# Two attentions of a four-layer kernel: products with the values in four blocks of one chunk of keys a group, in place of two blocks of two chunks

## What is computed

```python
# layer 2 (rope_ in the profile)
scores = einsum('bqhd,bkhd->bhqk', q, k) * scale
scores = where(causal, scores, -inf)
attn = softmax(scores, axis=-1)
ctx = einsum('bhqk,bkhd->bqhd', attn, v)
# layer 3 (ctx_ in the profile)
scores = einsum('bhqd,bhkd->bhqk', Q, K) * SCALE + 0.1 * influence[:, None]
attn = softmax(scores, axis=-1)
out = einsum('bhqk,bhkd->bhqd', attn, V)
```

## Time and profile before

| | |
|---|---|
| median of three runs | 1824.76 us (1817.14 to 1826.03) |
| the profiled execution | 1819.46 us, of which the span of instructions is 1817.7 |
| mean granted TensorE clock | 0.903 |
| TensorE matmuls busy | 1491.0 us (82%), 8757 records |
| TensorE weight loads busy | 881.8 us (49%) |
| VectorE busy | 1261.8 us (69%) |
| ScalarE busy | 1026.5 us (56%) |
| GpSimd busy | 825.7 us (45%) |
| products with the values, records | 1024 in rope, 1024 in ctx, all of L1717 |

### The profile page before, as it was taken

One profiled execution on the slowest core, in us unless ns is written; L12 is line 12 of the kernel. 1 busy time (PEld: TensorE's weight loads), 2 busy tenths in 40 slices (PEclk: granted clock), 3 DMA queues, 4 the chain that ended last, 5 costly groups with the idle time before them and its releaser, 6 DMA issues. The chain is left out here.

```text
span 1817.7 us, 26884 instructions
## 1 busy us (share of the span) xinstructions
PE 1491.0 (82%) x8757; PEld 881.8 (49%) x8757; DVE 1261.8 (69%) x3276; ACT 1026.5 (56%) x1749; POOL 825.7 (45%) x935
## 2 busy tenths in 40 slices
PE   3788888569998899587679999999995867999980
PEld 1444455334444444333245554555552745777770
DVE  1656667368888887368677777877872555888875
ACT  2444555326666666234546777767775634777762
POOL 1244534545666654425721121122002565688875
PEclk8889899769999999688869999999997878999995
DMA  7800000212222220000534444444420012344415
GB/s 210 269 14 1 1 1 1 61 56 76 72 76 70 71 75 25 17 1 1 114 86 128 124 106 108 120 120 122 98 50 24 21 60 84 116 125 138 128 54 139
DMA packets 104521, 143.77 MB, mean 79 GB/s; under 512 B 31906, under 2 KB 72867, under 8 KB 101808
## 3 DMA queue, kind: packets, MB, share of 16 engines
q1 hardware_dynamic: 99392, 133.59, 26.8%
q0 software_dynamic: 4992, 8.48, 1.4%
HBM read 103.93 MB, written 57.22 MB: 89 GB/s over the span
## 5 line engine op out<-in xcount | busy, mean ns | idle before, releaser
L1198 DVE TENSOR_REDUCE ctx_nm<-ctx_s 128x1 f32<-128x512 f32 x496 | 319.9, 680 | 87.1 <-PE ctx_s L1354 86.3
L1198 DVE TENSOR_REDUCE rope_nm<-rope_s 128x1 f32<-128x128 f32 x496 | 220.4, 479 | 63.1 <-PE rope_s L1357 61.4
L1598 ACT ACTIVATE rope_probs<-rope_st 128x1024 f32<-128x1024 f32 (+1 forms) x256 | 171.5, 702 | 122.8 <-PE rope_st L1701 121.4
L1598 ACT ACTIVATE ctx_probs<-ctx_st 128x1024 f32<-128x1024 f32 x192 | 190.3, 1023 | 87.1 <-PE ctx_st L1701 83.5
L1354 PE MATMUL ctx_s<-att_kst,att_qst 96*128 96x512 f32 x496 | 210.8, 458 | 19.3 <-DVE ctx_nm L1198 8.4
L1354 PE MATMUL rope_s<-att_kst,att_qst 96*128 96x128 bf16 x496 | 145.3, 312 | 25.9 <-DVE rope_nm L1198 12.7
L1701 PE MATMUL ctx_st<-att_qst,att_kst 98*128 98x512 f32 x512 | 164.4, 404 | 2.4 <-ACT ctx_probs L1598 1.5
L1354 PEld LDWEIGHTS ctx_s<-att_kst,att_qst 96*128 96x128 f32 x496 | 95.8, 193 | 126.9 <-DVE ctx_nm L1198 51.9
L1463 POOL TENSOR_SCALAR_AFFINE_SELECT rope_probs<-rope_probs 128x256 f32<-128x256 f32 x256 | 97.9, 410 | 114.9 <-ACT rope_probs L1598 113.8
L2970 DVE TENSOR_TENSOR sw_hf<-sw_silu,sw_u 128x512 f32<-128x512 f32 x124 | 84.6, 682 | 84.2 <-ACT sw_silu L2728 52.4
L2728 ACT ACTIVATE sw_silu<-sw_g 128x512 f32<-128x512 f32 x124 | 74.3, 599 | 117.7 <-PE sw_g L110 92.3
(11 more groups left out here) (435 smaller groups left out, 3507.0 us busy)
## 6 DMA issues: line engine op xcount, KB each, us to landing
sw_raw<-in_L_ffn_all SPq DMA_DIRECT2D x24, 768.0 KB
sw_xs<-in_pad SPq DMA_DIRECT2D x65, 260.0 KB, 10.6
ctx_halves<-att_qk SPq DMA_DIRECT2D x24, 512.0 KB, 5.7
att_qst<-ctx_contexts SPq DMA_DIRECT2D x32, 384.0 KB
att_kst<-ctx_contexts SPq DMA_DIRECT2D x32, 384.0 KB
rope_halves<-att_qk SPq DMA_DIRECT2D x32, 256.0 KB, 3.3
att_qst<-rope_halves SPq DMA_DIRECT2D x32, 192.0 KB, 3.0
att_kst<-rope_halves SPq DMA_DIRECT2D x32, 192.0 KB, 3.3
```

The lines of the kernel that those rows point to most:

```text
L1198: nc.vector.tensor_reduce(nm[:, g, j * T + t:j * T + t + 1], bank("s", b, n)[:, 0:keys], AXX, ALU.max, negate=True).then_inc(s_used, 1)
L1598: nc.scalar.activation(prob(n // GH % 2, n % GH)[:, u * units[0]:u * units[0] + units[u]], st_bank[u][:, 0:units[u]], ACT.Exp, scale=SCALE ...
```

## The change

`weigh_values` is called for chunk j after every odd step (h % 8 = 1, 3, 5, 7), one chunk each time, in place of chunks 0 and 1 after step 3 and chunks 2 and 3 after step 7. `weigh_values` itself, its waits, its increments and all other engines' programs stay as they are. The order among chunks is the same, so the sums are formed in the same order. The loop serves both attentions.

```diff
--- before.py
+++ after.py
@@ -1731,8 +1731,7 @@
                         scores_by_key(now[0], now[1] // 8, j, u)
                     if within(ahead[0]) and not lead(ahead):
                         score(*ahead, j, 2 * u + 1)
-                    if within(behind[0]) and u == 1 and j in (1, 3):
-                        weigh_values(*behind, j - 1)
+                    if within(behind[0]) and u == 1:
                         weigh_values(*behind, j)
                     if within(c) and c >= LEAD:
                         if h == AT["yT"]:
```

## The result

The changed kernel took 1811.88 us, the median of 13 runs (1802.87 to 1819.58), against 1819.7 (1814.51 to 1827.12, 13 runs) for the kernel before on the same chip: a ratio of 0.9949 (95% interval 0.9934 to 0.9964), 8 us less. The forecast was 20 us less. The sign was right, the size was not.

A forecast was written before the change was run, and what follows sets the result against it. TensorE and VectorE were taken to wait for each other in bursts. Borders of 4.7 us against 7.3 recovered (85% of 8.6) gave 2.6 a batch pair, times 7.75: -20 us, so 1800; forecast 1788 to 1814, range 1774 to 1830.

The forecast's parts named there:

- Ctx, borders: TensorE in ctx: each extra switch to 32-column matmuls and back costs 0.34 us, 2.7 us a batch for eight.
- Ctx, net -1.3 us a batch: Ctx attention: 2.7 us of added borders less 4.0 us of recovered TensorE stalls in each batch.
- the sum: Both stages over 7.75 batches: ctx -10, rope -20, -30 us in full; -20 us with 85% of recovery counted.
- Rope, borders: TensorE in rope: each extra switch of matmul mode and back costs 0.25 us, 2.0 us a batch.
- Rope, recovered 4.6 us a batch: TensorE in rope: the new blocks fill stalls for VectorE, the side bank and ScalarE, giving back 4.6 us a batch.
- The added wait, masks at step 1: Rope: the first chunk waits for GpSimd's last mask, 1.1 us once a batch, in place of a wait for VectorE.
- the rope term: Rope attention: net -2.6 us a batch, -20 us over 7.75 batches.
- 1 (borders tip the balance): Both attentions: waits move instead of shrinking, so extra borders become added time, 1834 to 1856 us; chance 0.14.
- 2: Rope: GpSimd's later masks hold two groups a batch about 1.2 us each, total 1811 to 1820 us; chance 0.17.
- 3: Both attentions: all waits between engines go, 12 us recovered a batch pair, about 1763 us; chance 0.06.
- 4: Whole kernel: nothing moves, time within 9 us of no change only by sums cancelling; chance 0.06.
- The signs: If right: VectorE's idle before scores down a third or more, batches about 43.5 (rope), 56.5 us (ctx); mask waits under 10.

The follow-up runs named there:

- borders_only: Kernel before, with one score tile placed between the two chunks of each value block in both attentions: +31.1 us, ratio 1.0183.
- ctx_only: Kernel before with one-chunk blocks in ctx alone, rope left as before: -11.4 us, ratio 0.9947.
- both_kfirst_masks: Changed kernel with the key stack loaded ahead of the guard and rope's last masks ahead of GpSimd's finish: -25.6 us against the kernel before, ratio 0.9850.
- before_kfirst: Kernel before with the key stack's load issued ahead of the guard's: -1.5 us, ratio 0.9992.
- ctx_kfirst: Kernel before with one-chunk blocks in ctx alone and key stacks loaded ahead of the guard: -15.4 us, ratio 0.9916.
- before_kfirst_2: Kernel before with the key stack's load ahead of the guard's, run again in a later group: -3.4 us, ratio 0.9977.
- rope_kfirst: Kernel before with one-chunk blocks in rope alone and key stacks loaded ahead of the guard: -7.3 us, ratio 0.9960.
- rope_only: Kernel before with one-chunk blocks in rope alone, ctx left as before: +3.2 us, ratio 1.0016.
- both_kfirst_masks_2: Changed kernel with early key stack load and rope's masks ahead of finish, run again: -28.4 us against the kernel before, ratio 0.9845.
- both_again: The changed kernel run once more for a second profile: -6.0 us against the kernel before, ratio 0.9968.
- both_kfirst: Changed kernel with the key stack's load issued ahead of the guard's: -20.7 us against the kernel before, ratio 0.9879.

## Why the prediction was right or wrong

1. *Ctx, borders* (0.34 us a pair): right, 0.337 after, 0.33 in borders_only.
2. *Ctx, net -1.3 us a batch*: right, though part of it needed the early load (loop -6 to -8 us without, -10 with). Typical periods of 56.1 to 56.5 against 57.57 are -1.1 to -1.5. The median of ctx_only, -11.4, lies beside the -10 in full of the sum. The half group of the earlier trace rows, 1165.35 to the block at 1169.14 and the score behind it at 1171.00, has its answer in the rows from 1163.35 to 1168.40: TensorE now has a block at 1163.35 where it stood still for VectorE.
3. *Rope, borders* (0.25): right in kind; borders_only's rope loop rose by 10 us for some 56 pairs, 0.18 each, and its typical period by 0.12 a pair, so part was covered.
4. *Rope, recovered 4.6 us a batch*: wrong, and this is the step that failed. It is so even with load and masks out of the way, where the typical period fell by 0.3 us (44.30 to 43.96 or 44.00) and not by 2.6. With eight pairs of borders at 0.12 (borders_only) to 0.25 us (the prediction's price) what came back is 1.3 to 2.3 us. Three things were wrong in the count. First, the items named in it sum to 3.9 at most (1.1 at 581.90, 1.0 at 595.34, three of 0.3, 0.9 before 607.25) and not to 4.6. Second, most of them did not go: TensorE's gaps in a quiet batch sum to 3.3 us before (491.71 to 536.01) and to 2.3 in both_kfirst_masks (487.33 to 531.33). The one of 0.95 for the side bank fell to 0.17, as foreseen, but the one of 0.67 for VectorE only to 0.59, and new ones of 0.24 and 0.26 for VectorE stand elsewhere. Third, the batch that I read was not typical. Distances between starts of L1253 in rope before are 43.2, 45.8, 44.3, 44.3 and 46.5 us; the quiet ones are 44.3 (all after the first in before_kfirst), and the one read was 45.78. The stall of 0.83 at 581.90, which I counted for every batch, occurs in two of them (the other at 447.53): VectorE's L1213 took 0.16 us in the batch before and 1.33 us in this one, while GpSimd ran a long operation (the order of time of VectorE twice, then of GpSimd, kernel before):

```profile
535.74 0.16 DVE L1213 TENSOR_TENSOR rope_cut<-rope_nm,rope_rounded 128x16 f32<-128x16 f32 x1
```

```profile
580.05 1.33 DVE L1213 TENSOR_TENSOR rope_cut<-rope_nm,rope_rounded 128x16 f32<-128x16 f32 x1
```

```profile
580.06 1.29 POOL L1107 TENSOR_TENSOR att_wide<-Y,att_twin 128x512 f32<-128x512 f32 x1
```

   Over rope's whole loop it is about 4 us less (303.3 and 305.5 against 308.2 to 308.9), where 2.6 x 7.75 = 20 was forecast. What sets 44.0 is open: VectorE was busy 152.1 of the 176.1 us of four batches (443.33 to 619.45 in both_kfirst_masks) and the weight loads of scores still waited 31.5 us for it.
5. *The added wait, masks at step 1 (1.1 us once a batch, hidden)*: place, size and cover right for a quiet batch. TensorE waits 0.73, 1.03, 0.73, 0.83 and 0.76 us at 480.71, 524.66, 568.21, 613.28 and 658.67 after, once a batch, where 1.1 was foreseen. The wait comes in place of one for VectorE (0.59 in both_kfirst_masks), and the typical period is the same with it and without. What wasn't foreseen is its cost outside of quiet batches: the slow clock behind some of these gaps, and 3 us or so at the end of the loop.
6. *What the sum didn't have*: the key stack's load. I followed what each engine waits for, and not what each would reach sooner. The step said of the moved products which waits come nearer (masks, bank, exponentials) and left out that shortening the block of chunks 2 and 3 at the group's end brings TensorE sooner to an operand whose load was 0.3 us from the edge before. It made 12 to 15 us of weight-load waits in rope and 5 to 9 us in ctx. It adds to the miss but isn't the step that failed: early loads take it away, and item 4 stays as it is. And not all of these waits cost time (see the periods after). The trace of before held the warning twice more, in waits of 5.29 us at 400.25 and of 1.11 at 625.06 for this very load:

```profile
400.25 0.29 PE L1354 MATMUL rope_s<-att_kst,att_qst 96*128 96x128 bf16 x1 [5.29 <-DMA att_kst<-rope_halves]
...
625.06 0.23 PE L1354 MATMUL rope_s<-att_kst,att_qst 96*128 96x128 bf16 x1 [1.11 <-DMA att_kst<-rope_halves]
```

7. *The total*: ctx -11, rope +3: -8. With the load early the kernel is 20.7 us under the one before, by chance the number forecast, with another split: ctx -12.0 (ctx_kfirst less before_kfirst_2), rope -3.9 (rope_kfirst less before_kfirst_2), the early load itself -1.5 to -3.4. It doesn't confirm the rope term.
8. *Rivals*: 1 (borders tip the balance) is false for ctx; rope alone is slower by a hair (+3.2, interval touching 1), but its typical period in rope_only is 43.96, so that comes with the waits for the load and the slow clock, not with the borders. 2 was the nearest to the result in time, 1811 to 1820, by luck: its wait is there, 0.7 to 1.1 us once a batch and not 2.4, and it was covered in quiet batches. 3 and 4 fell.
9. *The signs*: ctx's batch of 56.46, the pair of borders at 0.34 and 4.1 us of mask waits came as said. VectorE's idle time did not: it fell by 5% in rope (44.5 to 42.2) and 17% in ctx (73.9 to 61.2), where a third or more was named.

One difference is left open. By medians rope's change, with early load and masks, is worth 12.9 us (both_kfirst_masks_2 less ctx_kfirst), while its loop shows 4 to 5 us. About 4 of the missing 8 us are no time of the kernel: ctx_kfirst's profile is of its fastest execution (1782.56 us, 4.2 under its median). Of the 8.3 us between the two profiled executions 5.0 lie in rope's loop, 3.1 between rope's last score and ctx's first batch (228.6 and 225.5 us; 232.7 in before_kfirst_2) and 1.2 ahead of rope's loop, and ctx's loop and the rest give 1.0 back. These are differences of single profiles, and no run took the stretch between the loops apart. What the masks' move would give the kernel before was not tried either.

## What to carry to other kernels

When an edit makes an engine reach a point sooner, look at each operand of what stands next in its order and read how long before its use it landed: a load 0.3 us ahead of its user can be a wait after the edit. Read a gain from several periods of a stage, and take the most frequent, before you multiply one batch's stalls by the number of batches. And expect a gap that you fill to come back in part elsewhere: of 3.3 us of gaps in a quiet rope batch 1.0 went. And when two waits stand near each other, take both away before you judge either: early masks alone only lengthened the wait for the keys here, and with the early load they brought another 5 us by the medians.

## What the runs showed of the hardware

Short gaps of TensorE can be followed by a slower clock. After 0.94 and 0.73 us of idleness (565.97 and 568.21 above) a block of 512 columns took 1.94 us where the same block takes 1.06, and the three L1701 matmuls of 570.26 took 1.06 instead of 0.60. That is the lower of the clock's two levels, 1.2 in place of 2.4 GHz, and it lasted until 571.4, about 1.5 us of extra time (568.21 to 571.44 are 3.23 us, the same work from 480.71 to 482.44 took 1.73). The row of the stretch (columns as above) has a granted clock of 0.76:

```profile
565.00:572.00 7.00, 5.33 (x36) 2.50 (x33) 5.38 (x20) 2.87 (x5) 4.27 (x8) 0.76 0.12 32
```

But it is no rule that two such gaps do it. Two batches earlier in the same execution the same two gaps stand in the same places, and the block ran at the higher level:

```profile
478.48 0.23 PE L1354 MATMUL rope_s<-att_kst,att_qst 96*128 96x128 bf16 x1 [0.94 <-ACT rope_probs L1598]
...
480.71 1.06 PE L1717 MATMUL rope_out<-rope_probs,att_vaug 128*32 128x512 f32 x8 [0.73 <-POOL rope_probs L1463]
```

In five batches after, the mask gap came with a gap for the load in front of it each time, and the clock fell once. It fell twice more behind a single gap: at 434.9 (the block at 436.15 took 1.94 us) behind 2.44 us, and before 697.88 in one of 3.04. In both_again it fell four times: behind two gaps at 565.85 (1.73), and behind single ones of 1.69 (431.76), 1.60 (620.56) and 2.25 us (696.48), but not behind one of 1.88 (656.23), as it didn't behind the 1.82 at 623.06 after. In both_kfirst it fell behind two of the six mask gaps of about 1 us (606.74 and 691.69), each time with one of 0.55 us 2.4 us ahead. The kernel before has gaps of 0.95 and 0.67 us in every batch and one of 1.11 at 625.06, and none is followed by it. Over 413 to 700 us the granted clock was 1.00 before, 0.98 after, 0.97 in both_again and rope_only, 0.99 in both_kfirst, and 1.00 in both_kfirst_masks, where the gaps for load and masks are gone. So the gaps bring the risk of it; what decides in one case and not in the other these runs don't show. Three stretches of about 1.5 us each would be 4 to 5 us of rope's time after, an estimate from these rows that no run isolates.

VectorE's two-input operation of 0.16 us took 1.33 us when it met GpSimd's of 1.29, and ended with it. The Trainium skill (SBUF — State Buffer, Terms, shared port pair) says of the port pair of these two engines that it is locked for a whole instruction and the loser fully blocks. The rows agree, with 1.17 us of delay; TensorE's row behind it has a gap of 0.83 us, and the period of the other such meeting (445.68 us, no other long wait in it) is 45.77 us, 1.5 longer than a quiet one.
